# A transformer block on one core: a lead of 24 row-maxima tiles, filled in feed-forward turns 5 to 7, and the first sequence's projections a tile later

## The chip, the core and the metric

One core of one Trainium2 chip runs the whole program. Its engines are TensorE (PE in the profile, with its weight loads as PEld), VectorE (DVE), ScalarE (ACT), GpSimd (POOL) and the queue of SyncE (SP) that issues the DMAs. The metric is the device time of one execution, in microseconds; lower is better.

## What is computed

Eight sequences of 512 tokens and 256 channels pass through a feed-forward half step, an attention with 16 heads of 16 channels and an ALiBi bias, and the same feed-forward half step again:

```python
def _L0_ffn_ref(x, w_gate, w_up, w_down):
    gate = jnp.einsum('bsd,hd->bsh', x, wg)
    up = jnp.einsum('bsd,hd->bsh', x, wu)
    h = jax.nn.silu(gate) * up
    return jnp.einsum('bsh,dh->bsd', h, wd)
...
scores = jnp.einsum('bhld,bhsd->bhls', qh, kh) * inv_sqrt_d + bias[None]
attn = jax.nn.softmax(scores, axis=-1)
...
x = x + 0.5 * _L0_ffn_ref(_layernorm(x, axis=-1), L0_ffn_w_gate, L0_ffn_w_up, L0_ffn_w_down)
x = x + _L0_attn_ref(_layernorm(x, axis=-1), L0_attn_Wq, L0_attn_Wk, L0_attn_Wv, L0_attn_Wo, L0_attn_bo)
x = x + 0.5 * _L0_ffn_ref(_layernorm(x, axis=-1), L0_ffn_w_gate, L0_ffn_w_up, L0_ffn_w_down)
```

## The kernel before

The program has three stages, each of eight turns, one for each sequence `b`: the first feed-forward (`w` = 0), the attention, and the second feed-forward (`w` = 1). The order of the work is written out by hand for every engine, and semaphores join the engines.

**A feed-forward turn** (PE: `ffn_turn`, `gate_up`, `down`) has six tiles `f` of 128 hidden channels. For each, PE makes gate and up (eight products of 128x512), ACT applies Silu (`gated`, L560), DVE multiplies (`hid`, L759), and ACT and POOL split the result into a rounded and a rest part (L554, L459). Then come the down products, half of them, the eight transposes of the next turn's rows (`turn_x`, L967), and the other half. Those transposes go into PSUM banks 4 and 5 (`turn_at`). In between DVE does the next sequence's layernorm: `ln_gather` and `ln_links` (a chain of small Newton steps, L683 to L693), `ln_apply` (`xn`, L700) and `keep` (L707).

**An attention turn** has four quads `n` of four heads, and eight steps `s` in each. A step makes the scores of two heads against 128 keys (two products, from `q_aug` and `k_aug`), ACT's exponential (L647), POOL's multiplication with a table (L527), and in every second step the products with the values (`weigh_values`). Softmax needs the row maxima beforehand. They come from separate score tiles: `scores_for_max` makes a tile of 128 queries by 512 keys on PE, in turn in banks 4 and 5, and `row_maxima` reduces it on DVE (L824). A quad has 16 such tiles, a sequence 64. When a quad's sixteenth tile is reduced, DVE negates its 16 maxima in two small instructions (`negate`, L834 and L836). PE transposes them in the quad's `max` fill (L1011), ACT copies them to `max_row`, and two DMAs move them into `q_aug`, where the scores of that quad need them. A tile waits until DVE has reduced the tile two before it, which had the same bank.

**The lead.** The tiles run ahead of the scores: `MAX_LEAD` = 26 tiles ahead. The first 20 (`FIRST_MAX`) are made in the first feed-forward, in turns 6 and 7 (`FIRST_MAX_AT`, `FIRST_MAX_DOWN`), and sequence 0 makes three tiles a step until the lead is 26; from then on every step makes two.

```python
    ahead = MAX_LEAD + 2 * (step + 1)
    ahead = min(ahead, FIRST_MAX + 3 * (step + 1)) if b == 0 else ahead
```

**The fills** (`FILLS`, and `FIRST_AT` for sequence 0) are everything else of the attention on PE: transposes of the next rows (`xt`), projections (`qk`, `v`), transposes of heads and the output projection, at fixed steps; ACT drains each bank, and POOL or DVE splits it. Those of sequence 0 are done in turns 4 and 5 of the first feed-forward: its rows, kept in `heads` (L721), are transposed after a tile (`FIRST_TURN_AT`, L1079), ACT and DVE split them into `att_t` (L569, L776), and the first projections follow after later tiles.

Within attention step (n, s) DVE's order is: in quad 1, steps 2 to 5, one `xn` for a later sequence (`apply_kept`, L714), or for the last but one sequence the layernorm of sequence 0 (`first_rows`); then the maxima of the step, with a negation if a quad is complete; then `divide` (L888, L890) in step 4, or the split of `xt` (L880) in quad 0.

Of the kernel before, what the change touches and what calls it, by code (L numbers as in the profile page):

```python
# [82 lines left out]
def tables():  # L83
# [19 lines left out]
    for e in range(2):  # L103
# [25 lines left out]
FIRST_TURN_AT = (4, 0)  # L129
FIRST_AT = {(4, 3): "qk0_next", (4, 4): "qk1_next", (5, 0): "v0_next", (5, 1): "v1_next", (5, 2): "qk2_next", (5, 3): "qk3_next"}  # L130

FIRST_MAX_AT = {(B - 2, 0): range(0, 2), (B - 2, 2): range(2, 4), (B - 2, 4): range(4, 6),
                **{(B - 1, f): range(2 * f + 6, 2 * f + 8) for f in range(5)}}
FIRST_MAX_DOWN = {2: range(16, 18), 4: range(18, 20)}
FIRST_MAX = 20
# [17 lines left out]
MAX_LEAD = 26  # L153


def max_tiles_after(b, step):

    ahead = MAX_LEAD + 2 * (step + 1)
    ahead = min(ahead, FIRST_MAX + 3 * (step + 1)) if b == 0 else ahead
    return min(ahead, MAX_TILES) if b == B - 1 else ahead  # L160


def max_tiles_at(b, step):

    return range(max_tiles_after(b, step - 1), max_tiles_after(b, step))
# [30 lines left out]
def build_program(nc, d_x, d_wgu, d_wdn, d_watt, d_bo, d_qb, d_kb, d_diag, d_eye, d_scale, d_out):  # L196
    d_qrows = nc.dram_tensor("q_rows_scratch", (2, 2 * NSEG, NP, L), F32).ap()
    d_krows = nc.dram_tensor("k_rows_scratch", (ROWS - ROW_BIAS, L), F32).ap()
    with ExitStack() as ctx:
# [242 lines left out]
        def _(pool):  # L442
# [9 lines left out]
            def split_hidden(w, b):  # L452
# [10 lines left out]
                if w == 1 and first(b):  # L463
                    take(B, TAIL_AT[FT - 1])
                if w == 0 and first(b):
                    lay_ones()
# [79 lines left out]
        def _(act):  # L546
            def ffn_turn(w, b):
# [24 lines left out]
                hidden_hi(FT - 1)  # L572
                if w == 1 and first(b):
                    drain(B, TAIL_AT[FT - 1])
# [84 lines left out]
        def _(dve):  # L659
# [78 lines left out]
            def ffn_turn(w, b):  # L738
# [10 lines left out]
                for f in range(FT):  # L749
# [11 lines left out]

                    if f == 0 and w == 0 and not first(b):
                        ln_stats(1, b - 1, 2)
                        ln_stats(1, b - 1, 3)
# [8 lines left out]
                    if w == 0 and (b, f - 2) == FIRST_TURN_AT:  # L773
                        for k in range(KC):
                            dve.wait_ge(first_hi, k + 1)
                            nc.vector.tensor_tensor(att_t[:, 1, k, :], ps[:, turn_at + k, :], att_t[:, 0, k, :].bitcast(F32),  # L776
                                                    ALU.subtract).then_inc(first_split, 1)
# [175 lines left out]
        def _(pe):  # L953
# [25 lines left out]
            def fill(b, name, halves=(0, 1)):  # L979
# [27 lines left out]
                elif kind == "max":  # L1007
                    if halves[0] == 0:
                        pe.wait_ge(neg_ready, seq * NQ + part + 1)
                    if halves[0] == 0:  # L1010
# [22 lines left out]
            def scores_for_max(b, tiles):  # L1033

                for tile in tiles:
# [10 lines left out]
                    if seq == 0 and tile == 2 * STEPS:  # L1046
                        pe.wait_ge(drained, fill_no(-1, "max0_next") + 1)
# [163 lines left out]
```

## Time and profile before

| | |
|---|---|
| median of 3 runs | 893.54 us (890.49 to 893.92) |
| profiled execution | 892.85 us |
| its span | 891.1 us |
| mean granted clock | 0.97 |
| PE busy | 92% of the span |
| DVE busy | 73% |
| ACT, POOL busy | 58%, 48% |

The span goes from the first to the last instruction on the core. The granted clock is the share of TensorE's full clock of 2.4 GHz; 0.50 is the lower level of 1.2 GHz. A stretch from A to B is given in us from the start of the span: turn 4 goes from 104.86 to its down products at 125.40, quad 0 of sequence 0 from 197.43 to 223.32, quad 0 of sequence 3 from 406.13 and its quad 1 from 422.52 to 439.79, and quad 1 of sequence 4 from 488.30 to 506.77. PE 92% says that PE has something under way nearly always, not that it runs at its peak, and a share is a mean over three stages with different limits.

### The profile page before, as it was taken

What the parts mean: (1) busy time and instruction counts of PE and PEld (TensorE: products, weight loads), DVE (VectorE), ACT (ScalarE), POOL (GpSimd) and SP (SyncE); (2) the same over time, 40 slices, a digit from 0 to 9 for tenths busy, and PEclk for the clock granted to TensorE, in tenths of its full rate; (3) what the DMA queues carried; (4) which work ended last, traced back from release to release, by engine and by line L of the source; (5) the groups of instructions that cost most, each with busy time, mean ns of one, the idle gap of its engine ahead of it and who ended that gap; (6) DMA issues with size and microseconds to landing.
All of it is one profiled execution on the core that took longest, in us unless ns stands there. A gap on an engine that the chain in (4) does not pass through costs nothing.

```text
span 891.1 us, 13021 instructions
## 1 busy us (share of the span) xinstructions
PE 819.8 (92%) x4576; PEld 499.9 (56%) x4576; DVE 646.1 (73%) x1347; ACT 521.1 (58%) x745; POOL 425.6 (48%) x486
## 2 busy tenths in 40 slices
PE   2699989997899999999999999999899988999997
PEld 2578878763354453453444444444443436888886
DVE  5588877885787777777777777777878716777764
ACT  4343444334677777677777677677577773344443
POOL 0343345352544744744745645745554545344433
PEclk9799999996899999999999999999899999999999
DMA  9230015302532531531441541540522000010001
GB/s 362 103 40 3 2 29 78 41 11 31 72 50 26 72 54 21 72 54 20 72 60 15 73 60 15 72 66 12 69 43 31 2 3 1 32 44 26 26 25 50
DMA packets 21491, 43.18 MB, mean 48 GB/s; under 512 B 3848, under 2 KB 5912, under 8 KB 21208
## 3 DMA queue, kind: packets, MB, share of 16 engines
q1 hardware_dynamic: 21400, 41.92, 27.5%
q8 instruction: 63, 1.03, 0.5%
q14 instruction: 28, 0.23, 0.1%
HBM read 12.02 MB, written 4.62 MB: 19 GB/s over the span
## 4 chain that ended last, share of the span: by engine, by line
PE 65%; DVE 18%; DMA 4%; ACT 4%; issue 4%; POOL 2%; SPq 2%; DVEq 0%; ACTq 0%
PE ps L955 60%; DVE row_max L824 7%; DVE hid L759 3%; DMA q_aug<-max_row 2%; DMA q_scale<-q_scale 2%; PE ps L1016 2%; ACT stage L605 2%; PE ps L967 1%; DVE xnt L880 1%; ACT xnt L611 1%; DVE newton L691 1%; DVE xn L714 1%; DVE var L683 1%; PE ps L993 1%; POOL x_sb L510 1%
## 5 line engine op out<-in xcount | busy, mean ns | idle before, releaser
L824 DVE TENSOR_REDUCE row_max<-ps 128x1 f32<-128x512 f32 x512 | 329.3, 685 | 105.9 <-PE ps L955 104.5
L647 ACT ACTIVATE probs<-ps 128x1024 f32<-128x1024 f32 x256 | 259.9, 1026 | 48.9 <-PE ps L955 48.4
L527 POOL TENSOR_TENSOR probs<-probs,diag 128x256 f32<-128x256 f32 x256 | 186.5, 732 | 193.6 <-ACT probs L647 193.5
L459 POOL TENSOR_TENSOR hid_r<-hid,hid_r 128x512 fp32r<-128x512 f32 x96 | 124.8, 1301 | 196.1 <-ACT hid_r L554 195.2
L955 PE MATMUL ps<-xnt,wgu_r 128*128 128x512 f32 x768 | 195.8, 409 | 17.3 <-DVE hid L759 13.0
L955 PE MATMUL ps<-k_aug,q_aug 60*128 60x512 f32 x512 | 163.5, 448 | 19.6 <-DVE row_max L824 14.6
L955 PEld LDWEIGHTS ps<-xnt,wgu_r 128*128 128x128 f32 x768 | 145.9, 194 | 59.2 <-DVE hid L759 18.2
L955 PE MATMUL ps<-probs,v_aug 128*32 128x512 f32 x1024 | 141.9, 627 | 7.0 <-POOL probs L527 7.0
L560 ACT ACTIVATE gated<-ps 128x512 f32<-128x512 f32 x96 | 57.3, 598 | 141.4 <-PE ps L955 132.2
L955 PE MATMUL ps<-q_aug,k_aug 62*128 62x512 f32 x512 | 131.3, 505 | 3.8 <-DMA q_aug<-max_row 3.4
L955 PEld LDWEIGHTS ps<-k_aug,q_aug 60*128 60x128 f32 x512 | 81.0, 190 | 73.1 <-DVE row_max L824 66.5
L955 PEld LDWEIGHTS ps<-q_aug,k_aug 62*128 62x128 f32 x512 | 49.1, 187 | 116.1 <-issue 70.6
L759 DVE SCALAR_TENSOR_TENSOR hid<-ps,gated 128x512 f32<-128x512 f32 x96 | 65.9, 687 | 56.4 <-PE ps L955 28.7
L955 PE MATMUL ps<-wdn_r,hid_r 128*128 128x256 f32 x768 | 97.4, 282 | 0.9 <-ACT stage L605 0.9
L955 PEld LDWEIGHTS ps<-wdn_r,hid_r 128*128 128x128 f32 x768 | 93.8, 188 | 3.0 <-issue 1.6
L605 ACT COPY stage<-ps 128x512 f32<-128x512 f32 x96 | 56.3, 586 | 52.6 <-PE ps L955 28.9
L554 ACT CAST hid_r<-hid 128x512 fp32r<-128x512 f32 x96 | 59.1, 615 | 21.3 <-DVE hid L759 21.2
L483 POOL TENSOR_TENSOR parts<-stage,parts 128x512 fp32r<-128x512 f32 x32 | 41.2, 1286 | 35.7 <-ACT parts L611 35.7
L955 PEld LDWEIGHTS ps<-probs,v_aug 128*32 128x32 f32 x1024 | 20.4, 109 | 47.2 <-issue 24.7
L955 PE MATMUL ps<-xnt,wqkv 128*128 128x512 f32 x168 | 46.6, 413 | 0.0
L700 DVE TENSOR_SCALAR xn<-x_sb,mean_var,rstd 128x256 f32<-128x256 f32 x64 | 38.2, 622 | 0.5
L663 DVE BATCH_NORM_STATS2 stats<-x_sb 128x6 f32<-128x256 f32 x96 | 34.1, 410 | 5.4 <-DMA x_sb<-x_in 5.4
(72 smaller groups left out, 656.9 us busy)
## 6 DMA issues: line engine op xcount, KB each, us to landing
q_aug<-parts SPq DMA_DIRECT2D x96, 128.0 KB, 4.2
k_aug<-parts SPq DMA_DIRECT2D x96, 128.0 KB, 6.0
x_sb<-x_in SPq DMA_DIRECT2D x8, 512.0 KB, 12.7
x_out<-x_sb SPq DMA_DIRECT2D x8, 512.0 KB, 2.6
diag<-diag_table SPq DMA_DIRECT2D x1, 2048.0 KB, 18.8
wgu_i<-w_gate_up SPq DMA_DIRECT2D x2, 768.0 KB, 6.0
w_att<-w_att SPq DMA_DIRECT2D x1, 1024.0 KB, 11.2
q_aug<-max_row SPq DMA_DIRECT2D x64, 8.0 KB
```

What stands on the lines that cost most here:

```text
L459: nc.gpsimd.tensor_tensor(hid_r[:, 1, f, :], hid[:, f % 2, :], hid_r[:, 0, f, :].bitcast(F32), ALU.subtract).then_inc(s["hid_lo"], 1)
L483: nc.gpsimd.tensor_tensor(lo, stage[:, slot_of(b, name), :], hi.bitcast(F32), ALU.subtract).then_inc(done[SPLIT_POOL], 1)
L527: nc.gpsimd.tensor_tensor(tile, tile, diag[:, kt % 2, n * QH + 2 * pair:n * QH + 2 * pair + 2, :], ALU.mult).then_inc(fixed, 1)
L554: nc.scalar.copy(hid_r[:, 0, f, :], hid[:, f % 2, :]).then_inc(s["hid_hi"], 1)
L560: nc.scalar.activation(gated[:, f % 2, :], ps[:, gate_at + f % 2, :], ACT.Silu, scale=DEQ).then_inc(s["gated_ready"], 1)
L605: nc.scalar.copy(stage[:, slot_of(b, name), :], bank).then_inc(drained, 1)
L647: nc.scalar.activation(probs[:, kt % 2, 2 * pair:2 * pair + 2, :], ps[:, at:at + 2, :], ACT.Exp, scale=SLOPE_UNITS[pair]).then_inc(exp_don ...
L663: nc.vector.bn_stats(stats[:, slot, tile, :], x_of(b, tile)).then_inc(ln_step, 1)
L700: nc.vector.tensor_scalar(xn[:, tile, :], x_of(b, tile), mean_var[:, 0, tile, 0:1], rstd[:, 0, tile:tile + 1], ALU.subtract, ALU.mult).the ...
L759: nc.vector.scalar_tensor_tensor(hid[:, f % 2, :], ps[:, up_at + f % 2, :], DEQ, gated[:, f % 2, :], ALU.mult, ALU.mult).then_inc(s["hid_r ...
L824: nc.vector.reduce_max(row_max[:, quad % 2, u % 2, u // STEPS, (u % STEPS) // 2:(u % STEPS) // 2 + 1], max_bank(tile), mybir.AxisListType. ...
L955: return nc.tensor.matmul(out, lhs, rhs, start=start, stop=stop, **k)
```

## The change

Four things, on several engines:

1. `FIRST_TURN_AT` goes from (4, 0) to (4, 1), and the first two projections of sequence 0 from after tiles 3 and 4 to after tiles 4 and 5 of turn 4. POOL and ACT get a place for the drain of a fill after a turn's last tile.
2. DVE's half of that split comes straight after `hid` of tile 3, ahead of the layernorm's links; before, it came after `hid` of tile 2 and the links behind that.
3. `MAX_LEAD` is 24, and all of it is made in the first feed-forward: two tiles after the last tile of turn 5, six in turn 6, twelve after the six tiles of turn 7 and four among its down products. No step makes three tiles.
4. The first transpose of maxima waits until the tiles before the down products are reduced, since their bank is its own.

```diff
-FIRST_TURN_AT = (4, 0)
-FIRST_AT = {(4, 3): "qk0_next", (4, 4): "qk1_next", (5, 0): "v0_next", (5, 1): "v1_next", (5, 2): "qk2_next", (5, 3): "qk3_next"}
+FIRST_TURN_AT = (4, 1)
+FIRST_AT = {(4, 4): "qk0_next", (4, 5): "qk1_next", (5, 0): "v0_next", (5, 1): "v1_next", (5, 2): "qk2_next", (5, 3): "qk3_next"}
...
-FIRST_MAX_AT = {(B - 2, 0): range(0, 2), (B - 2, 2): range(2, 4), (B - 2, 4): range(4, 6),
-                **{(B - 1, f): range(2 * f + 6, 2 * f + 8) for f in range(5)}}
-FIRST_MAX_DOWN = {2: range(16, 18), 4: range(18, 20)}
-FIRST_MAX = 20
+FIRST_MAX_AT = {(B - 3, 5): range(0, 2), (B - 2, 0): range(2, 4), (B - 2, 2): range(4, 6), (B - 2, 4): range(6, 8),
+                **{(B - 1, f): range(2 * f + 8, 2 * f + 10) for f in range(FT)}}
+FIRST_MAX_DOWN = {2: range(20, 22), 4: range(22, 24)}
...
-MAX_LEAD = 26
...
+MAX_LEAD = 24
...
-    return range(max_tiles_after(b, step - 1), max_tiles_after(b, step))
+    made = MAX_LEAD + 2 * step
+    return range(made, min(made + 2, MAX_TILES) if b == B - 1 else made + 2)
...
                     nc.vector.scalar_tensor_tensor(hid[:, f % 2, :], ps[:, up_at + f % 2, :], DEQ, gated[:, f % 2, :],
                                                    ALU.mult, ALU.mult).then_inc(s["hid_ready"], 1)
 
+                    if w == 0 and (b, f - 2) == FIRST_TURN_AT:
+                        for k in range(KC):
+                            dve.wait_ge(first_hi, k + 1)
+                            nc.vector.tensor_tensor(att_t[:, 1, k, :], ps[:, turn_at + k, :], att_t[:, 0, k, :].bitcast(F32),
+                                                    ALU.subtract).then_inc(first_split, 1)
...
+                        if b < 0:
+                            pe.wait_ge(s1_used, FIRST_MAX_DOWN[2][0])
```

How the orders move. In turn 4, DVE, from `hid` of tile 2 on. Before:

```order
L759 SCALAR_TENSOR_TENSOR hid<-ps,gated 128x512
L691 TENSOR_TENSOR newton<-newton,var 128x8
L693 SCALAR_TENSOR_TENSOR rstd<-newton,rstd 128x8
L689 SCALAR_TENSOR_TENSOR newton<-rstd 128x8
L691 TENSOR_TENSOR newton<-newton,var 128x8
L693 SCALAR_TENSOR_TENSOR rstd<-newton,rstd 128x8
L776 TENSOR_TENSOR att_t<-ps,att_t 128x512 x2
L759 SCALAR_TENSOR_TENSOR hid<-ps,gated 128x512
```

And after the change, from the same `hid`, which is L756 there:

```order
L756 SCALAR_TENSOR_TENSOR hid<-ps,gated 128x512
L688 TENSOR_TENSOR newton<-newton,var 128x8
L690 SCALAR_TENSOR_TENSOR rstd<-newton,rstd 128x8
L686 SCALAR_TENSOR_TENSOR newton<-rstd 128x8
L688 TENSOR_TENSOR newton<-newton,var 128x8
L690 SCALAR_TENSOR_TENSOR rstd<-newton,rstd 128x8
L756 SCALAR_TENSOR_TENSOR hid<-ps,gated 128x512
L762 TENSOR_TENSOR att_t<-ps,att_t 128x512 x2
```

The two splits of `att_t` have moved behind the `hid` of tile 3.

At the end of turn 5, DVE, after the last `xn`. After the change:

```order
L697 TENSOR_SCALAR xn<-x_sb,mean_var,rstd 128x256
L704 TENSOR_SCALAR kept_mean<-mean_var 128x4
L704 TENSOR_SCALAR kept_rstd<-rstd 128x4
L821 TENSOR_REDUCE row_max<-ps 128x1 x2
L660 BN_STATS stats<-x_sb 128x6 x4
L726 TENSOR_TENSOR xnt<-ps,xnt 128x512 x2
```

The pair of reductions is new there; the rest is the order of before.

In every attention turn, DVE, in quad 1, from its `xn` of step 2 to its `xn` of step 5. Before:

```order
L714 TENSOR_SCALAR xn<-x_sb,kept_mean,kept_rstd 128x256
L824 TENSOR_REDUCE row_max<-ps 128x1 x2
L834 TENSOR_SCALAR max_in<-row_max 128x2x8
L836 SCALAR_TENSOR_TENSOR max_in<-row_max,max_in 128x2x8
L714 TENSOR_SCALAR xn<-x_sb,kept_mean,kept_rstd 128x256
L824 TENSOR_REDUCE row_max<-ps 128x1 x2
L714 TENSOR_SCALAR xn<-x_sb,kept_mean,kept_rstd 128x256
L824 TENSOR_REDUCE row_max<-ps 128x1 x2
L888 RECIPROCAL den<-stage 128x16
L890 TENSOR_TENSOR heads<-stage,den 128x4x64
```

After the change:

```order
L711 TENSOR_SCALAR xn<-x_sb,kept_mean,kept_rstd 128x256
L821 TENSOR_REDUCE row_max<-ps 128x1 x2
L711 TENSOR_SCALAR xn<-x_sb,kept_mean,kept_rstd 128x256
L821 TENSOR_REDUCE row_max<-ps 128x1 x2
L831 TENSOR_SCALAR max_in<-row_max 128x2x8
L833 SCALAR_TENSOR_TENSOR max_in<-row_max,max_in 128x2x8
L711 TENSOR_SCALAR xn<-x_sb,kept_mean,kept_rstd 128x256
L821 TENSOR_REDUCE row_max<-ps 128x1 x2
L885 RECIPROCAL den<-stage 128x16
L887 TENSOR_TENSOR heads<-stage,den 128x4x64
```

The negation (L834 and L836, now L831 and L833) stands behind the maxima of step 3 instead of those of step 2. It does so in all four quads.

## Rows read from the trace of the kernel before

**Rows 1.** The page, busy time, share of the span and instructions by engine.
```profile
PE 819.8 (92%) x4576; PEld 499.9 (56%) x4576; DVE 646.1 (73%) x1347; ACT 521.1 (58%) x745; POOL 425.6 (48%) x486
```
**Rows 2.** The page, the chain that ended last, shares by engine.
```profile
PE 65%; DVE 18%; DMA 4%; ACT 4%; issue 4%; POOL 2%; SPq 2%; DVEq 0%; ACTq 0%
```
**Rows 3.** Stretches: width; busy PE, PEld, DVE, ACT, POOL; PEclk, DMA share, GB/s.
```profile
104.86:125.40 20.54, 16.90 (x70) 13.08 (x69) 13.43 (x38) 7.85 (x15) 5.17 (x4) 0.92 0.01 2
197.43:223.32 25.89, 19.90 (x78) 8.12 (x77) 16.56 (x28) 11.09 (x15) 5.50 (x9) 0.74 0.28 34
406.13:422.52 16.39, 15.43 (x85) 6.74 (x85) 12.04 (x22) 11.94 (x17) 7.14 (x13) 1.00 0.00 1
422.52:439.79 17.27, 16.40 (x97) 7.71 (x93) 14.00 (x25) 12.54 (x17) 13.04 (x16) 1.00 0.62 93
488.30:506.77 18.47, 17.59 (x96) 7.78 (x93) 13.99 (x25) 12.55 (x17) 13.05 (x16) 0.91 0.63 87
```
**Rows 4.** Timeline of turn 4: start, duration, engine, work, idle time before and its releaser.
```profile
107.66 1.09 PE L1079 MATMUL ps<-eye,heads 128*128 128x128 f32 x8 [0.77 <-DVE heads L721]
115.87 1.28 DVE L776 TENSOR_TENSOR att_t<-ps,att_t 128x512 fp32r<-128x512 f32 x2
117.20 2.43 PE L955 MATMUL ps<-att_t,wqkv 128*128 128x512 f32 x6 [2.86 <-DVE att_t L776]
119.43 2.85 PE L955 MATMUL ps<-xnt,wgu_r 128*128 128x512 f32 x8
122.12 1.57 PE L955 MATMUL ps<-att_t,wqkv 128*128 128x512 f32 x6
123.53 2.03 PE L955 MATMUL ps<-xnt,wgu_r 128*128 128x512 f32 x8
```
**Rows 5.** Timeline, end of turn 5, and a pair of reductions in turn 6.
```profile
151.59 1.04 PE L967 MATMUL ps<-eye,xn 128*128 128x128 f32 x8
152.47 0.16 DVE L707 TENSOR_SCALAR kept_rstd<-rstd 128x4 f32<-128x4 f32 x1
168.71 1.27 DVE L824 TENSOR_REDUCE row_max<-ps 128x1 f32<-128x512 f32 x2
```
**Rows 6.** Timeline, turn 7, from tile 5 to the down products.
```profile
190.33 0.27 PE L1011 MATMUL ps<-eye,max_in 128*32 128x128 f32 x1
190.37 0.69 DVE L759 SCALAR_TENSOR_TENSOR hid<-ps,gated 128x512 f32<-128x512 f32 x1 [0.19 <-PE ps L955]
```
**Rows 7.** Timeline, PE, steps 0 and 1 of sequence 0.
```profile
199.45 0.49 PE L955 MATMUL ps<-k_aug,q_aug 60*128 60x512 f32 x1 [1.28 <-DVE row_max L824]
203.18 0.79 PE L955 MATMUL ps<-k_aug,q_aug 60*128 60x512 f32 x1 [1.96 <-DVE row_max L824]
```
**Rows 8.** Timeline, sequence 3, quad 0, steps 2 to 4.
```profile
412.06 0.17 DVE L834 TENSOR_SCALAR max_in<-row_max 128x16 fp32r<-128x16 f32 x1
412.27 0.17 DVE L836 SCALAR_TENSOR_TENSOR max_in<-row_max,max_in 128x16 f32<-128x16 f32 x1
413.80 2.56 DVE L824 TENSOR_REDUCE row_max<-ps 128x1 f32<-128x512 f32 x4
415.25 0.73 POOL L527 TENSOR_TENSOR probs<-probs,diag 128x256 f32<-128x256 f32 x1
```
**Rows 9.** Timeline, sequence 3, quad 1, steps 2 to 5.
```profile
429.25 0.65 DVE L836 SCALAR_TENSOR_TENSOR max_in<-row_max,max_in 128x16 f32<-128x16 f32 x1
430.52 1.33 POOL L483 TENSOR_TENSOR att_t<-stage,att_t 128x512 fp32r<-128x512 f32 x1
432.61 1.27 DVE L824 TENSOR_REDUCE row_max<-ps 128x1 f32<-128x512 f32 x2
433.34 1.09 PE L955 MATMUL ps<-k_aug,q_aug 60*128 60x512 f32 x2
```
**Rows 10.** Timeline, sequence 3, quad 2, the reductions of steps 3 and 4.
```profile
447.20 1.29 DVE L824 TENSOR_REDUCE row_max<-ps 128x1 f32<-128x512 f32 x2 [0.56 <-PE ps L955]
448.85 1.29 DVE L824 TENSOR_REDUCE row_max<-ps 128x1 f32<-128x512 f32 x2 [0.37 <-PE ps L955]
```

More of the change, by code:

```diff
@@ L152 @@
 MAX_TILES = 2 * NQ * STEPS
-MAX_LEAD = 26
[L156 to L160, printed above, removed]
+MAX_LEAD = 24
 def max_tiles_at(b, step):
-    return range(max_tiles_after(b, step - 1), max_tiles_after(b, step))
+    made = MAX_LEAD + 2 * step
+    return range(made, min(made + 2, MAX_TILES) if b == B - 1 else made + 2)
 SPLIT_POOL, SPLIT_DVE, HEADS, OUT = ("qk", "turn"), ("xt",), ("heads",), ("out",)
@@ L464, in split_hidden @@
                     take(B, TAIL_AT[FT - 1])
+                if w == 0 and (b, FT - 1) in FIRST_AT:
+                    take(-1, FIRST_AT[b, FT - 1])
                 if w == 0 and first(b):
@@ L572, in ffn_turn @@
                 hidden_hi(FT - 1)
+                if w == 0 and (b, FT - 1) in FIRST_AT:
+                    drain(-1, FIRST_AT[b, FT - 1])
                 if w == 1 and first(b):
@@ L772, in ffn_turn @@
                         keep(at, b - 1, 1)
[L773 to L777, printed above, removed]
                     if w == 0 and (b, f) in FIRST_MAX_AT:
@@ L1045, in scores_for_max @@
                         pe.wait_ge(drained, fill_no(-1, "qk3_next") + 1)
-                    if seq == 0 and tile == 2 * STEPS:
+                    if seq == 0 and tile == FIRST_MAX_DOWN[2][0]:
                         pe.wait_ge(drained, fill_no(-1, "max0_next") + 1)
```

## The prediction

> **What bounds the kernel now.** I read first the page's busy shares: PE has 92% of the span and DVE 73% [rows 1], so time is won or lost where PE stands still or is slowed, and DVE matters where PE waits for it. The chain that ended last says the same, 65% PE and 18% DVE [rows 2]. Busy time by stretches comes next [rows 3]. Quad 0 of sequence 0, the first stretch of the attention, takes 25.89 us at a granted clock of 0.74. The same quad of sequence 3 takes 16.39 us at 1.00, with more fills in it. Feed-forward turn 4, as far as its down products, takes 20.54 us at 0.92, while DVE is busy for 13.43. These are the places that the change aims at. Everything else that it moves is in the negations, so last I followed DVE in the timeline round three of them.
>
> The sum is made against the profiled execution: span 891.1, time 892.85. The median of the runs shown is 893.54, 0.69 more, and I add that at the end. About 0.5% (4.5 us) is what a measurement of this kernel can tell from no change.
>
> **Turn 4: transposes after f=1, first projection after f=4, the split ahead of the Newton links.** Now PE waits 0.77 for the rows of sequence 0, then 2.86 for the split `att_t`, and after that wait it runs at the lower level (1.2 GHz of 2.4): six products take 2.43 and eight 2.85, against 1.57 and 2.03 for the same work at the higher one [rows 4]. Together 0.77 + 2.86 + 0.86 + 0.82 = 5.3. After the change the rows have been ready for a turn's tile, and the split follows `hid` of f=3 directly. PE has the eight products of f=4 in between, 2.03 long as those at 123.53; DVE needs 1.28 for the two splits behind `hid`, and may start late by the links of f=2. I leave a wait of 0.5: **-4.8** (ends -3.5, were the links as late as now, and -5.3).
>
> **Turn 5: two tiles after f=5.** The transposes of turn 6 go into the same PSUM banks, so they now wait until DVE has reduced both tiles. Those two reductions stand behind `kept_mean` and `kept_rstd`, the last of which starts at 152.47 and takes 0.16; with 1.27 for a pair of reductions they end at about 153.9. The transposes start at 151.59 now [rows 5]. The two score products, ahead of the down products, are inside that wait. **+2.4** (ends 0.5, the products alone, and 3.0). Behind the transposes wait ACT's and DVE's halves of `xnt` and then gate and up of turn 6; those have the second half of the down products as cover, and would add the time of a reduction pair if it were too short.
>
> **Turn 7: two tiles after f=5, and the first transpose of the maxima behind them.** That transpose (L1011) writes the bank of those tiles and newly waits for 20 reductions. DVE's `hid` of f=5 starts at 190.37 and takes 0.69 [rows 6], a pair of reductions 1.27 more, so PE is let go at about 192.4 instead of 190.33. With rounding and semaphores **+2.2** (ends 0.5 and 2.6). Behind it on PE are all down products of the turn. SP's move of the maxima shifts with it and still lands before the attention starts.
>
> **Quad 0 of sequence 0: two tiles a step instead of three.** PE waits for the third tile's bank, 1.28 in step 0 and 1.96 in step 1, and behind the second wait a product takes 0.79 against 0.49 before: the lower level of the clock [rows 7]. Six such tiles leave the quad, each a product on PE and a reduction on DVE. I followed the steps with durations of the rows: DVE stays the one that is waited for in steps 1 to 5 (two splits of `xnt` wait for ACT), and the quad comes out at 16.9 us with the clock up. It isn't likely to stay up: steps 0 to 2 still hold no value products, and PE stands still for about 1.3 us for tiles 28 and 29. I add 2.5 for slow stretches and take 19.4, so **-6.5**. Ends: -9.0 with the clock up, -2.9 if it behaves as now.
>
> **Every quad: the negation goes from step 2 to step 3.** A lead of 24 makes the sixteenth tile of a quad in step 3. The first instruction of a negation takes 0.17 when POOL is idle, and so does the second; reductions, which read PSUM, keep 0.64 under POOL's operations too [rows 8]. But where POOL is under way the second takes 0.65, and it ends as POOL's operation ends [rows 9]. `xn` (L714) waits in the same way. So a negation costs what is left of POOL's operation.
> - Quad 0: in step 2 it sits in a gap in which DVE waits for ACT's half of `xt1`; it costs nothing there. In step 3 it falls between four reductions that follow one another, under POOL's operations, the last of them until 415.98 [rows 8]. The reductions of step 4 start 0.9 later; PE, which needs them in step 5, catches up a part at step 6, where it waited for DVE before. +0.4, seven times: 2.8.
> - Quad 1: DVE loses the negation ahead of step 3's reductions, which PE does not need so early (its value products wait for POOL there), and gets it ahead of step 4's. Those start at 432.61 now, and PE issues step 5's first tile at 433.34 right behind the first of them [rows 9]. If the first half just misses the start of POOL's 1.33 us operation at 430.52, they start 0.8 later; if it catches it, not at all. By my times it misses by 0.05. +0.6 for each of sequences 0 to 5: 3.6.
> - Quads 2 and 3: DVE is idle for 0.56 between step 2's negation and step 3's reductions, and for 0.37 ahead of step 4's [rows 10]. The negation now has to go into those 0.37, and needs 0.34 alone and more under POOL. +0.2, fourteen times: 2.8.
> - Sequence 6, quad 1, where the negation is ahead of a long chain: -0.3. Sequence 7, quad 1: +0.2. Two more tiles in step 19 of the last sequence, otherwise bound by ACT: +0.3.
>
> Together **+9.4**. Ends: 1.5, if DVE's slack covers nearly all, and 15. What holds DVE off in these rows is POOL's operation, to its end. The Trainium skill, GPSIMD Engine Reference, "1. Specifications", says only that GpSimd's SBUF interfaces are shared with those VectorE instructions that have two SBUF inputs or run in a two-port mode, and names no turn-taking. Priced by that sentence without the rows, a moved negation would be its own 0.34, largely inside the gaps, and the sum of this part 3 instead of 9.4. The trace agrees with the page on which instructions suffer and goes beyond it on how long.
>
> **Sum.** -4.8 + 2.4 + 2.2 - 6.5 + 9.4 = +2.7; 892.85 + 2.7 = 895.6, and with the 0.69 of the median **896.3**.
>
> **The rivals.**
> - *Faster: DVE's slack covers the negations.* Quad 1's negation catches the boundary, the other quads absorb theirs, and sequence 0 starts with the clock up. For it: PE's waits for reductions are short in most steps, and 0.05 us decide in quad 1. Against: the gap of 0.37 in quad 2 is shorter than the negation with its wait. -4.8 + 2.4 + 2.2 - 9.0 + 1.5 = -7.7: 885.8.
> - *Slower: quad 1 loses the clock.* With step 5's tiles held by the negation, PE has a second weak stretch right behind the one at POOL's wait in step 3. Quad 1 of sequence 4 shows what follows: 18.47 us at 0.91 against 17.27 at 1.00 in sequence 3 [rows 3], 1.2 us. It decides once quad 1's wait before step 5 grows by about 0.8. Three more sequences so, and the quad late every time (2.5 more): +2.7 + 3.6 + 2.5 = +8.8: 902.3.
> - *The start doesn't come free.* Quad 0 of sequence 0 keeps its slow stretches, since DVE's wait for ACT's halves of `xnt` stays: -2.9 instead of -6.5, so +6.3: 899.8. The wait for three tiles was then not what set those steps.
>
> **How the numbers follow.** Forecast 0.38, the faster rival 0.28, quad 1's clock 0.22, the start 0.12. The forecast lies within 0.5%; the two rivals above it are slower by more. So faster 0.28, same 0.38, slower 0.34. The likeliest case's own range is 889 to 898.5; the range over all goes to a little beyond both outer rivals, 885 to 904. The clock falls in other places too (sequences 2, 4 and 6 now), and these may come or go by 3 us with no cause in the change; it is inside the range.
>
> **What would show it.** Turn 4 to its down products near 15.7 us. A PE wait of some 2 us before turn 6's transposes, and one of 1.6 before the first L1011 (L1010 there). Quad 0 of sequence 0 between 17 and 20 us. Quad 0 of sequences 1 to 6 at 16.8 instead of 16.39, quad 1 at 17.3 to 18.2, quads 2 and 3 up by 0.2; negation instructions of 0.4 to 1.3 us in step 3. If the steady quads are unchanged to 0.1, the forecast is wrong by the whole of its largest term and the kernel is faster. If quad 0 of sequence 0 is over 23 us, the extra tile wasn't what slowed it.

## The result and the profile after

| | time, us | clock of the runs |
|---|---|---|
| before, 4 runs beside it | 892.01 (889.68 to 893.92) | |
| after, 4 runs | 901.7 (898.82 to 907.14) | 0.967, 0.967, 0.958, 0.961 |
| after, the profiled execution | 898.82, span 896.9 | 0.967 |

The ratio is 1.0121, with a 95% interval of 1.0076 to 1.0167: the change makes the kernel slower. Ten more runs, made later and told below (e11), gave 897.38 us and 1.0053 (1.0029 to 1.0078). So the forecast of 896.3 lies 5.4 us under the first measurement and 1.1 under the second, and both lie in the range of 885 to 904; only the second lies in the likeliest case's own range, 889 to 898.5. As a difference from the kernel before the forecast does less well: +2.8 was forecast, and +9.7 and +5.2 were measured.

The page of the profile after, busy time by engine and the chain that ended last, against [rows 1, 2]:

```profile
PE 823.9 (92%) x4576; PEld 500.8 (56%) x4576; DVE 645.0 (72%) x1347; ACT 519.7 (58%) x745; POOL 426.5 (48%) x486
PE 61%; DVE 25%; DMA 4%; issue 4%; ACT 3%; SPq 2%; POOL 1%; DVEq 0%; ACTq 0%
```

All counts of instructions are the same, and DVE works no longer. Yet the chain goes through DVE for 25% of the span instead of 18%: work has moved to where it is waited for.

The stretches of the profile after, with the columns of [rows 3] (width; busy PE, PEld, DVE, ACT, POOL; granted clock, DMA share, GB/s). In order: turn 4; turn 7 before and after the first transpose of the maxima; quad 0 of sequence 0; quads 0 and 1 of sequence 1, then of sequence 3:

```profile
104.92:120.69 15.77, 15.13 (x71) 12.01 (x70) 14.05 (x40) 8.00 (x15) 6.14 (x5) 1.00 0.01 2
186.00:189.60 3.60, 1.91 (x10) 1.12 (x9) 2.62 (x5) 1.72 (x3) 2.40 (x3) 1.00 0.02 5
189.60:193.00 3.40, 3.40 (x19) 3.17 (x17) 0.00 (x0) 1.54 (x2) 3.19 (x5) 0.50 0.02 5
197.95:216.23 18.28, 15.66 (x72) 6.53 (x72) 12.72 (x22) 10.88 (x15) 5.54 (x9) 0.81 0.40 48
264.91:281.66 16.75, 15.65 (x88) 6.66 (x85) 12.45 (x22) 12.04 (x18) 7.71 (x14) 1.00 0.01 2
281.66:299.44 17.78, 16.02 (x97) 7.53 (x93) 14.52 (x25) 12.45 (x17) 13.20 (x16) 1.00 0.69 89
400.16:418.34 18.18, 17.16 (x85) 6.83 (x85) 12.38 (x22) 11.95 (x17) 7.20 (x14) 0.91 0.01 2
418.34:436.11 17.77, 16.02 (x97) 7.52 (x93) 14.50 (x25) 12.45 (x17) 13.17 (x16) 1.00 0.67 90
```

Turn 4 has lost 4.77 us and has its full clock. Quad 0 of sequence 0 has lost 7.61, though its clock is still 0.81. Against that, a steady quad 0 takes 16.75 in sequence 1 at full clock and 18.18 in sequence 3, where the clock is 0.91 (before: 16.39 at 1.00). All of sequences 2 to 6 look like sequence 3: 18.16 to 18.21. Quad 1 takes 17.78 in place of 17.27 and keeps its clock in sequences 1 to 5 (in sequence 6, where it had lost it before, it takes 22.96 at 0.78 against 22.35 at 0.85). And turn 7, which had no such stretch before, has 3.4 us at the lower level.

**Where the 5.8 us of span went**, by the starts of the sequences (the first exponential of each) in the two profiled executions:

| part | before | after | difference | predicted |
|---|---|---|---|---|
| up to sequence 0 | 197.4 | 197.9 | +0.5 | -0.2 |
| sequence 0 | 75.8 | 67.0 | -8.8 | about -5.5 |
| sequences 1 to 6 | 402.4 | 412.9 | +10.5 | about +7.5 |
| sequence 7 | 50.2 | 52.7 | +2.5 | about +0.9 |
| after it | 165.3 | 166.4 | +1.1 | 0 |

What sequences 1 to 7 lose is more than what the freed start had saved. Of the other three executions after, one was as long as this one, and two were longer, at lower clocks (0.958 and 0.961).

**The steps in the trace.** The timeline of the profile after (start, duration, engine, work, idle time before and its releaser), turns 4, 5 and 7:

```profile
114.59 1.28 DVE L762 TENSOR_TENSOR att_t<-ps,att_t 128x512 fp32r<-128x512 f32 x2
115.93 1.66 PE L952 MATMUL ps<-att_t,wqkv 128*128 128x512 f32 x6 [0.64 <-DVE att_t L762]
...
146.59 1.25 DVE L704 TENSOR_SCALAR kept_mean<-mean_var 128x4 f32<-128x4 f32 x1
147.75 0.16 DVE L704 TENSOR_SCALAR kept_rstd<-rstd 128x4 f32<-128x4 f32 x1
147.82 1.27 DVE L821 TENSOR_REDUCE row_max<-ps 128x1 f32<-128x512 f32 x2
149.20 1.06 PE L964 MATMUL ps<-eye,xn 128*128 128x128 f32 x8 [1.54 <-issue]
...
187.95 1.28 DVE L821 TENSOR_REDUCE row_max<-ps 128x1 f32<-128x512 f32 x2
189.38 0.27 PE L1010 MATMUL ps<-eye,max_in 128*32 128x128 f32 x1 [1.70 <-DVE row_max L821]
189.40 3.61 PE L952 MATMUL ps<-wdn_r,hid_r 128*128 128x256 f32 x16
```

The split in turn 4 now costs PE 0.64 instead of 2.86 [rows 4]. In turn 5 PE stands still for 1.54 us until the pair of reductions is through, and that pair stands behind a copy of four numbers a row that took 1.25 us. In turn 7 PE waits 1.70 us. The sixteen down products behind it took 3.61, at the lower level.

The same view, DVE, POOL and PE in steps 3 to 5 of sequence 3, quad 0 and then quad 1, against [rows 8, 9]:

```profile
409.13 0.20 DVE L831 TENSOR_SCALAR max_in<-row_max 128x16 fp32r<-128x16 f32 x1
409.27 0.73 POOL L522 TENSOR_TENSOR probs<-probs,diag 128x256 f32<-128x256 f32 x1
409.37 0.66 DVE L833 SCALAR_TENSOR_TENSOR max_in<-row_max,max_in 128x16 f32<-128x16 f32 x1
409.96 1.27 DVE L821 TENSOR_REDUCE row_max<-ps 128x1 f32<-128x512 f32 x2
...
426.38 1.32 DVE L831 TENSOR_SCALAR max_in<-row_max 128x16 fp32r<-128x16 f32 x1
426.38 1.28 POOL L478 TENSOR_TENSOR att_t<-stage,att_t 128x512 fp32r<-128x512 f32 x1
427.73 0.65 DVE L833 SCALAR_TENSOR_TENSOR max_in<-row_max,max_in 128x16 f32<-128x16 f32 x1
428.63 1.28 DVE L821 TENSOR_REDUCE row_max<-ps 128x1 f32<-128x512 f32 x2
429.36 1.10 PE L952 MATMUL ps<-k_aug,q_aug 60*128 60x512 f32 x2 [0.84 <-DVE row_max L821]
```

In quad 0 the second negation instruction runs from 409.37 to 410.03 and ends with POOL's operation, at 410.00. In quad 1 the first starts together with POOL's 1.28 us operation and takes 1.32: it just missed the boundary, as the prediction had it. The reductions of step 4 start at 428.63, and PE waits 0.84 for them.

What this does to PE is seen best in a quad 0 at full clock. PE, from step 4's transposes on, in sequence 3 before and in sequence 1 after:

```profile
416.14 0.50 PE L955 MATMUL ps<-q_aug,k_aug 62*128 62x512 f32 x2
416.48 0.42 PE L955 MATMUL ps<-k_aug,q_aug 60*128 60x512 f32 x2
416.83 1.07 PE L955 MATMUL ps<-probs,v_aug 128*32 128x512 f32 x8
418.04 0.50 PE L955 MATMUL ps<-q_aug,k_aug 62*128 62x512 f32 x2
```

```profile
275.00 0.50 PE L952 MATMUL ps<-q_aug,k_aug 62*128 62x512 f32 x2
275.51 1.09 PE L952 MATMUL ps<-k_aug,q_aug 60*128 60x512 f32 x2
276.53 1.07 PE L952 MATMUL ps<-probs,v_aug 128*32 128x512 f32 x8
277.74 0.50 PE L952 MATMUL ps<-q_aug,k_aug 62*128 62x512 f32 x2
```

The value products start 1.53 us after step 5's scores instead of 0.69, because the two maxima tiles ahead of them (`k_aug`) are issued as reductions free their banks. Step 5 takes 2.74 instead of 1.90; step 6 gives back 0.55.

What PE did ahead of a fall is seen in the stretch from step 4's scores to step 5's value products: in sequence 3 after, where the clock fell at 411.5, inside step 5; in sequence 1 after, where it did not; and in sequence 3 before (columns as above):

```profile
407.53:411.88 4.35, 3.57 (x16) 1.51 (x12) 4.25 (x10) 3.08 (x4) 1.77 (x4) 0.95 0.00 0
272.36:276.53 4.17, 3.39 (x16) 1.52 (x12) 4.07 (x9) 2.99 (x4) 1.76 (x3) 1.00 0.01 2
413.50:416.83 3.33, 2.69 (x16) 1.42 (x12) 2.85 (x5) 2.15 (x4) 1.75 (x3) 1.00 0.00 0
```

The same twelve products (the count of PE takes in four that are just ending) take 0.84 us longer in sequence 1 than before (4.17 against 3.33), with no value products among them. Sequence 1 has this thin stretch and keeps its clock, so the stretch by itself doesn't decide whether the clock falls.

### The profile page after: what moved, and what is told of

Same layout as the page of the kernel before. It is cut to its first block, busy times and chain, and to the rows that moved or that the text cites. A ratio compares the mean times of both kernels' runs of the same rounds, so it can differ in the third digit from the quotient of the medians.

```text
span 896.9 us, 13022 instructions
## 1 busy us (share of the span) xinstructions
PE 823.9 (92%) x4576; PEld 500.8 (56%) x4576; DVE 645.0 (72%) x1347; ACT 519.7 (58%) x745; POOL 426.5 (48%) x486
## 3 DMA queue, kind: packets, MB, share of 16 engines
q1 hardware_dynamic: 21400, 41.92, 27.3%
## 4 chain that ended last, share of the span: by engine, by line
PE 61%; DVE 25%; DMA 4%; issue 4%; ACT 3%; SPq 2%; POOL 1%; DVEq 0%; ACTq 0%
PE ps L952 57%; DVE row_max L821 12%; DVE hid L756 3%; DMA q_aug<-max_row 2%; DMA q_scale<-q_scale 2%; DVE max_in L831 2%; PE ps L964 1%; ACT stage L602 1%; DVE max_in L833 1%; DVE xnt L877 1%; ACT xnt L608 1%; DVE newton L688 1%; DVE xn L711 1%; PE ps L1010 1%; PE ps L990 1%
## 5 line engine op out<-in xcount | busy, mean ns | idle before, releaser
L952 PEld LDWEIGHTS ps<-k_aug,q_aug 60*128 60x128 f32 x512 | 78.4, 191 | 75.4 <-DVE row_max L821 62.9
L756 DVE SCALAR_TENSOR_TENSOR hid<-ps,gated 128x512 f32<-128x512 f32 x96 | 65.8, 687 | 51.4 <-PE ps L952 31.7
L660 DVE BATCH_NORM_STATS2 stats<-x_sb 128x6 f32<-128x256 f32 x96 | 34.1, 409 | 5.5 <-DMA x_sb<-x_in 5.5
```

Of the source, the lines that this page charges most:

```text
L660: nc.vector.bn_stats(stats[:, slot, tile, :], x_of(b, tile)).then_inc(ln_step, 1)
L756: nc.vector.scalar_tensor_tensor(hid[:, f % 2, :], ps[:, up_at + f % 2, :], DEQ, gated[:, f % 2, :], ALU.mult, ALU.mult).then_inc(s["hid_r ...
L952: return nc.tensor.matmul(out, lhs, rhs, start=start, stop=stop, **k)
```

## The experiments

Eleven kernels and the change once more, all with 6 to 12 runs each. Nearly every one was slower or faster partly by its clock, so I use one measure beside the ratio. Every run has a span and a mean granted clock; **slow time** is what it spent at the lower level, 2 x span x (1 - clock). Over the 74 runs of the kernel before that stood beside the experiments, a microsecond of slow time goes with 0.32 us of span; within the runs of all kernels together with 0.34. Span less a third of the slow time, the **rest**, then varies by only 0.4 to 1.3 us (standard deviation) within a kernel. The third is fitted to these runs and no law; the clock is given to 0.001, which is 1.8 us of slow time. A fall in a steady quad 0 costs more than a third, 1.5 us for 3.4 (18.18 against 16.68), so the rest of a kernel with many such falls still holds some clock.

| kernel | runs | ratio | mean span | slow time | rest |
|---|---|---|---|---|---|
| before | 74 | 1 | 890.4 | 50.5 | 873.6 |
| after, first measurement | 4 | 1.0121 | 900.4 | 66.2 | 878.4 |
| after, again (e11) | 10 | 1.0053 | 896.0 | 54.5 | 877.8 |
| turn 4 alone (e1) | 12 | 0.9947 | 886.0 | 48.4 | 869.9 |
| negation late, lead 26 (e2) | 6 | 1.0137 | 901.8 | 66.2 | 879.8 |
| late in quad 0 alone (e9) | 6 | 1.0116 | 900.9 | 67.3 | 878.5 |
| late in quad 1 alone (e10) | 12 | 1.0024 | 893.1 | 53.0 | 875.5 |
| change with lead 26 (e3) | 6 | 0.9904 | 882.3 | 34.1 | 870.9 |
| e3 with both waits cut (e8) | 6 | 0.9903 | 881.5 | 35.3 | 869.7 |
| change, negation in step 4 (e4) | 12 | 0.9969 | 887.3 | 37.4 | 874.9 |
| change without turn 5's pair (e5) | 7 | 1.0066 | 895.8 | 54.0 | 877.8 |
| change, pair ahead (e6) | 12 | 1.0040 | 894.0 | 52.5 | 876.5 |
| change, transpose later (e7) | 12 | 1.0012 | 892.1 | 48.5 | 876.0 |
| change, e6 and e7 together (e12) | 12 | 1.0021 | 892.4 | 49.1 | 876.1 |

### The change taken apart

**e1: only turn 4's part, on the kernel before.** The six lines of `FIRST_TURN_AT`, `FIRST_AT` and the split and drain that belong to them; 20 tiles and lead 26 stay.

> The kernel before with the change's turn 4 alone (transposes after f=1, the split behind hid of f=3, the first projections after f=4 and f=5). Main theory: turn 4 to its down products goes from 20.5 us to 15.7, as in the changed kernel, nothing else moves, so about 887.2 us against 892.0, ratio 0.995, with 1 us either way by where the clock falls. Rival (turn 4's gain is lost to what follows it): the attention starts as late as before and the ratio is 1.00.

888.08 us, ratio 0.9947 (0.9928 to 0.9966). The attention starts at 192.8 instead of 197.4. Quad 0 of sequence 0 is no shorter, 27.3. The part is worth what was predicted (-4.8; measured -4.5 on the median), and all of it reaches the end.

**e2: only the negation a step later, on the kernel before.** Lead 26 stays, so nothing but the place of two small DVE instructions changes:

```diff
-                        row_maxima(b, max_tiles_at(b, n * STEPS + s))
+                        row_maxima(b, max_tiles_at(b, n * STEPS + s), False)
+                        if s == 3 and not (last(b) and n == NQ - 1):
+                            negate(b * NQ + n + 1, (n + 1) % 2)
```

> The kernel before, lead 26, with one thing altered: each negation of the attention stands behind the maxima of step 3 instead of step 2, where the tile is complete. Main theory (the place of the negation on DVE is what costs, not the lead): quad 0 of sequences 1 to 6 goes from 16.4 to 16.75 us at full clock and to 18.2 where the clock falls, quad 1 from 17.3 to 17.8, together 7 to 12 us, 899 to 904 us, ratio 1.008 to 1.014. Rival (the shorter lead costs, since tiles and negation come later against the scores that need them, or the waits put into turns 5 and 7): the steady quads stay at 16.4 and 17.3 and the ratio is within 1.002.

903.43 us, ratio 1.0137 (1.0094 to 1.0181): 10.9 us for moving two instructions of 0.17 us per quad. At full clock quad 0 takes 16.7 and quad 1 17.8, as in the change, and quads 2 and 3 are unchanged at 16.1. The rest is up 6.2 us. The other part is clock: 15.7 us more of slow time. Its profiled execution, the fastest of the six, shows only one fall in a quad 0 (sequence 2, 19.7 us), so where the others lost their clock is not seen here; e9 shows it better.

**e3: the change, but with lead 26.** The first 24 tiles as in the change, then three tiles in steps 0 and 1 of sequence 0, so that a quad's sixteenth tile stays in step 2 and the negation with it:

```diff
-MAX_LEAD = 24
+MAX_LEAD = 26
+FIRST_MAX = 24
...
+    ahead = MAX_LEAD + 2 * (step + 1)
+    ahead = min(ahead, FIRST_MAX + 3 * (step + 1)) if b == 0 else ahead
```

> The changed kernel with its first 24 tiles and turn 4 kept, but lead 26: steps 0 and 1 of sequence 0 make three tiles, all later ones two, so that every negation is back behind step 2. Main theory: steady quads as before (16.4, 17.3, falls of the clock as before), the first feed-forward as in the changed kernel (attention starts near 198), quad 0 of sequence 0 near 19.5 us against 25.9: 892.0 + 0.5 - 6.4 = 886, ratio 0.993. Rival (the negations are innocent; three tiles a step or the turns' waits cost): quad 0 of sequence 0 back over 23 us and 890 or more, or steady quads still at 18.2.

884.26 us, ratio 0.9904 (0.9875 to 0.9933), the best of the study together with e8. Its stretches (quad 0 of sequence 0; quads 0 and 1 of sequence 3):

```profile
198.25:218.06 19.81, 15.79 (x76) 6.86 (x75) 13.99 (x24) 11.00 (x15) 5.54 (x9) 0.83 0.36 45
398.32:414.71 16.39, 15.43 (x83) 6.73 (x84) 12.04 (x22) 11.92 (x17) 7.08 (x13) 1.00 0.01 2
414.71:431.96 17.25, 16.39 (x95) 7.70 (x91) 13.98 (x25) 12.57 (x17) 13.04 (x16) 1.00 0.69 93
```

The steady quads are those of before [rows 3], and the long quad 0 of the start is gone: 19.8 instead of 25.9, with the three-tile steps still in it. So it was four more steps of three tiles that made it long, and the change's lead of 24 isn't needed for the gain. Against e1 the slow time is 14 us less and the rest 1 us more. Put together, e3 and e2 give 0.9904 x 1.0137 = 1.004 for the whole change (an estimate, which leaves out the tail's +1.4 us and the two three-tile steps that e3 still has): the second measurement of the change has that in its interval, the first doesn't.

**e4: the change, negation behind step 4's maxima.** The diff of e2 on the changed kernel, with `s == 4`.

> The changed kernel, lead 24, with each negation of the attention behind the maxima of step 4, ahead of divide, still ahead of the fill in step 5 that needs it. Main theory: in quad 0 DVE waits for ACT at that place anyway, so quad 0 is back at 16.4 us without a fall of the clock; quad 1 is freed ahead of step 4's maxima and pays ahead of step 5's instead, 17.3 to 17.7; together 8 us less than the changed kernel, about 892 to 894, ratio 1.000 to 1.003. Rival (the lead is what costs): quad 0 stays at 16.75 to 18.2 and the time near 901.

889.68 us, ratio 0.9969 (0.9950 to 0.9989), faster than expected. In sequence 3 quad 0 is back at 16.4 and quad 1 at 17.4; quad 2 takes 16.5 in place of 16.15. So step 3 is the bad place, and a lead of 24 doesn't need it. It isn't free, though: quad 2 of sequence 7 still takes 13.43 instead of 12.06, by the two more tiles that a shorter lead leaves for the end, and e4 stays 5.4 us over e3.

### Which quad

**e9 and e10: the negation late in one quad only, on the kernel before.** In e9 the test of e2 reads `n == 0`, in e10 `n == 1`, and the other quads negate in step 2.

> The kernel before (lead 26), with the two negation instructions moved behind step 3's maxima in quad 0 alone; in quads 1 to 3 they stay in step 2. Theory (the 0.3 us that quad 0 loses in steps 5 and 6, on top of the kernel's other waits, is what lets the clock fall there): quad 0 takes 16.7 at full clock and up to 19.6 with a fall, quad 1 stays at 17.3, and at least half of the slowdown of the full move (1.0137) is seen, ratio 1.006 to 1.010. Rival (quad 1's loss of 0.5 us under GpSimd's long operation carries it): ratio under 1.003.

> The kernel before (lead 26), with the two negation instructions moved behind step 3's maxima in quad 1 alone. Theory: quad 1 takes 17.8 (from 17.3), that is 7 x 0.5 = 3.5 us or 0.4%, and no more, as the falls of the clock belong to quad 0: ratio 1.003 to 1.005. Rival (quad 1 loses the clock by itself, the slower rival of the prediction): ratio 1.008 or above, with falls in quad 1's steps 5 and 6 in most sequences.

e9: 902.75 us, 1.0116 (1.0084 to 1.0149). e10: 894.74 us, 1.0024 (1.0005 to 1.0043). Stretches of e9 (quad 0 of sequences 1 and 2, quad 1 of sequence 2) and of e10 (quads 0 and 1 of sequence 1, then of sequence 2):

```profile
275.11:291.94 16.83, 15.69 (x88) 6.65 (x84) 12.56 (x22) 12.11 (x18) 7.77 (x14) 1.00 0.01 2
341.30:359.45 18.15, 17.15 (x84) 6.84 (x84) 12.41 (x22) 11.66 (x16) 7.25 (x13) 0.91 0.01 2
359.45:376.95 17.50, 16.46 (x95) 7.73 (x92) 14.26 (x25) 12.83 (x18) 13.10 (x16) 1.00 0.71 92
```

```profile
272.97:289.51 16.54, 15.44 (x88) 6.73 (x85) 12.19 (x22) 12.10 (x18) 7.80 (x14) 1.00 0.01 2
289.51:308.03 18.52, 17.05 (x97) 7.56 (x93) 14.55 (x25) 12.45 (x17) 13.06 (x16) 0.91 0.66 86
340.23:356.62 16.39, 15.44 (x83) 6.73 (x83) 12.03 (x22) 11.65 (x16) 7.21 (x13) 1.00 0.01 3
356.62:374.67 18.05, 16.33 (x95) 7.58 (x91) 14.84 (x25) 12.74 (x18) 13.10 (x16) 1.00 0.69 89
```

Quad 0 decides. With only 0.3 us lost there at full clock (0.85 in sequence 7) it brings 16.8 us of slow time more and nearly the whole slowdown of e2; in its profile quad 0 took 18.2 in sequences 2, 3, 5 and 6, at 0.91 in each. That is more than my theory gave it (1.006 to 1.010). Its rest is up by 4.9 where those losses at full clock make 2.7, since these falls cost more than a third. Quad 1, which loses 0.5 us at full clock, brings 2.5 us of slow time; the clock fell in it in sequences 1 and 5 (18.5 and 18.5), and in sequences 2 and 4 of the kernel before (18.2 and 18.5). So quad 1 is not where the slowdown comes from, as the slower rival had it. What quad 1 does when quad 0 is late as well, as in the change, these two don't show.

### The waits in the feed-forward

**e5: the change without turn 5's pair**, with 22 tiles in the feed-forward turns and three tiles in steps 0 and 1 of sequence 0.

> The changed kernel without the pair of maxima tiles in turn 5 (22 tiles in the feed-forward turns, three tiles instead of two in steps 0 and 1 of sequence 0, lead still 24). My theory of turn 5 (the pair and the wait of the next turn's transposes cost about +2.2 there): attention starts at about 195.8 us instead of 197.95, and quad 0 of sequence 0 takes 18.9 instead of 18.3, so the ratio to the kernel before is about 0.2% under the change's 1.0121, near 1.010. Rival (the wait in turn 5 hides in turn 6 or 7): the start stays at 197.9 and the ratio is 1.012 or above. Both: the clock still falls once in quad 0 of nearly every later sequence, since the negation is where the change puts it.

897.05 us, 1.0066 (1.0035 to 1.0098). The attention starts at 194.2, earlier than my 195.8 (no fall in turn 7 here), and quad 0 of sequence 0 takes 19.6, for my 18.9. In its profile the clock fell in quad 0 of sequences 2, 4, 5 and 7, not of nearly all. The rest equals that of the change: what turn 5 saves, the three-tile steps cost.

**e6: the pair's reductions ahead of the two copies.**

```diff
-                    if 1 in slots and f == 5:
-                        keep(at, b - 1, 1)
                     if w == 0 and (b, f) in FIRST_MAX_AT:
                         row_maxima(0, FIRST_MAX_AT[b, f])
+                    if 1 in slots and f == 5:
+                        keep(at, b - 1, 1)
```

> The changed kernel with the turn-5 pair's row maxima put ahead of the two copies of kept mean and reciprocal on VectorE (0.6 to 1.3 us of queue). Theory (the maxima wait behind the copies, and TensorE waits for the maxima): the idle stretch ahead of turn 5's transposes goes from 1.54 us to about 0.2, attention starts at about 196.6, and the whole is 1.3 us shorter than the change. Rival (another wait, such as the drain of v0_next or GpSimd's port, takes the place): the idle stretch is 1 us or more still.

Timeline of e6, turn 5:

```profile
146.45 1.28 DVE L821 TENSOR_REDUCE row_max<-ps 128x1 f32<-128x512 f32 x2
147.65 0.16 DVE L704 TENSOR_SCALAR kept_mean<-mean_var 128x4 f32<-128x4 f32 x1
147.72 1.25 DVE L704 TENSOR_SCALAR kept_rstd<-rstd 128x4 f32<-128x4 f32 x1
147.83 1.07 PE L964 MATMUL ps<-eye,xn 128*128 128x128 f32 x8 [0.32 <-issue]
```

The idle time falls from 1.54 to 0.32, as expected, though the attention starts at 197.1 for my 196.6 (the clock fell in turn 7); the copies still take 1.25 between them, now with nobody waiting. 895.80 us, 1.0040 (1.0016 to 1.0064); the rest is 1.3 us under e11's.

**e7: the first transpose of the maxima one tile later** (`f == 1` instead of `f == 0` in `down`).

> The changed kernel with the transpose of sequence 0's first maxima one f-tile later in turn 7's down products (f = 1 instead of f = 0). Theory (that transpose waits 1.7 us for the last row maxima, and the idle stretch with the products around it brings the clock to 0.5 for 3.4 us): the wait is under 0.8 us, the stretch at 189.6 to 193.0 is at full clock, and attention starts 1.5 to 2.5 us sooner (about 195.9). Rival A (the clock falls for another reason, such as the small products of turn 7): the wait shrinks and the fall stays, attention starts about 1 us sooner. Rival B (moving rows is late then): quad 0 of sequence 0 takes over 18.5 us.

Timeline of e7, turn 7:

```profile
188.04 1.20 PE L952 MATMUL ps<-wdn_r,hid_r 128*128 128x256 f32 x8
189.81 0.27 PE L1010 MATMUL ps<-eye,max_in 128*32 128x128 f32 x1 [0.56 <-DVE row_max L821]
```

The wait is 0.56 instead of 1.70 and no fall follows; the attention starts at 195.98. 894.26 us, 1.0012 (0.9988 to 1.0036), the rest 1.8 us under e11's. But the absence of the fall doesn't show that the wait caused it: e11, with the wait as it was, has none in turn 7 either, and e6 has one.

**e8 and e12: both edits together**, on e3 and on the change.

> The version with lead 26, 24 tiles made in the feed-forward turns and the later turn 4 (measured 0.9904 of the kernel before), with the turn-5 maxima ahead of the copies and the transpose of the first maxima one f-tile later. If both waits are what they seem, another 1.3 and 1.5 to 2.5 us go: about 881 us, ratio 0.987. If the start of the attention part only waits for something else then (rows that move, first maxima), the ratio stays at 0.990. The steady quads stay at 16.4 and 17.3, with no fall of the clock in quad 0.

> The changed kernel (lead 24) with both edits on waits: turn 5's row maxima ahead of the two copies, and the transpose of the first maxima one f-tile later in turn 7. If the gains add, attention starts 3 to 3.5 us sooner than in the change (about 194.7) and the ratio is 1.004 or less below that of the change measured beside it by at least 0.35%. If the time in the later part goes by where the falls of the clock land, the ratio can be anywhere from 0.998 to 1.007 whatever the start gained.

e8: 883.22 us, 0.9903 (0.9868 to 0.9937), 1.0 us under e3 and no difference that these runs can tell; the expected 881 wasn't reached. e12: 894.73 us, 1.0021 (0.9999 to 1.0044); its attention starts at 194.5, 3.5 us before that of the change's first profile and 1.5 before that of e11 (196.0), its rest is 1.7 us under e11's, and it is no better than e7 alone. The gains of the two don't add up in the time, and I didn't find out why.

**e11: the change again.**

> The changed kernel as it is, again, beside the others on the same chip. Its ratio was 1.0121 from four runs with 1.0 to 1.3% spread, while the three variants of it that shorten the wait in turn 5 or 7 by 1 to 4 us gave 1.0012 to 1.0066. If the variants gained by more than their own waits (fewer falls of the clock later on), this run gives 1.009 or above; if the first measurement lay high, 1.006 to 1.009.

897.38 us (894.36 to 903.55), 1.0053 (1.0029 to 1.0078): below both ranges that I had set. The rest is the same as in the first measurement to 0.6 us, the slow time 12 us less. Its profiled execution shows the falls otherwise placed. Stretches, quad 0 of sequences 2 and 3, quads 0 and 1 of sequence 4:

```profile
327.70:347.23 19.53, 18.61 (x83) 7.71 (x83) 12.38 (x22) 11.66 (x16) 7.43 (x13) 0.83 0.01 2
397.57:414.25 16.68, 15.62 (x83) 6.65 (x83) 12.38 (x22) 11.92 (x17) 7.21 (x14) 1.00 0.01 2
464.21:483.75 19.54, 18.59 (x83) 7.71 (x83) 12.37 (x22) 11.93 (x17) 7.35 (x14) 0.83 0.00 1
483.75:503.97 20.22, 18.56 (x95) 8.73 (x91) 14.50 (x25) 12.45 (x17) 13.24 (x16) 0.83 0.57 80
```

Here the clock falls for twice as long in quad 0, 6.8 us, and only in sequences 2, 4 and 5 (and for 3.4 in 7). And it falls in quad 1: for 6.8 us in sequences 4 and 5, where quad 1 takes 20.2, and for 17.1 in sequence 6, where it takes 24.9 against 22.35 before. The profiles of e5, e6 and e7, which have late negations in every quad too, also show falls in quad 1, in two to four of sequences 1 to 5; in e7 quad 1 of sequence 1 takes 20.5 right behind a quad 0 at full clock (16.8). So the slower rival's falls in quad 1 do come in the change, though not in every execution, and though e10 gives quad 1 by itself only 0.24%. No run has quads 0 and 1 late and the others not, so what the two do together isn't taken apart. The change has a cost at full clock and one that differs from execution to execution.

## Why the prediction was right and wrong

By its own steps, for the profiled executions:

- **Turn 4, -4.8: right.** 15.77 us to the down products for a forecast of 15.7; the wait for the split 0.64 for 0.5; e1 carries it to the end of the program.
- **Turn 5, +2.4: right in mechanism, a little high.** From the start of the down products to that of the transposes it is 4.63 us, against 2.84 before: +1.8, and 0.43 for the two score products, together +2.2. The term's copy of `kept_mean` stands where it was put, and e6, which moves it away, wins 1.3 in the rest.
- **Turn 7, +2.2: the wait was right, the clock was missed.** PE's wait of 1.70 was forecast as 1.6. Behind it sixteen down products took 3.61 us in place of the 2.15 that they take at full clock: another 1.45, which no term had. In e11 it didn't come.
- **Quad 0 of sequence 0, -6.5: right, and 1.1 too small**: 18.28 us for 19.4; 17.2 in e11, and 18.2 in e7.
- **The negation step, +9.4: the sum came out near, 11.8, and its make-up didn't.** (11.8 is +13.0 in sequences 1 to 7, less 1.2 in quads 1 to 3 of sequence 0.) At full clock the pieces add up to about 7 only (2.6 in quad 0, 2.9 in quad 1, 1.4 in the tail); that falls of the clock made up for what the term had too much is luck. *Quad 0* was given +0.4. At full clock it is +0.23 in sequence 1 (16.75 for 16.52), +0.29 in sequence 3 of e11 (16.68 for 16.39) and +0.86 in the last sequence, so the price of the wait holds. But in five sequences of the profile the clock fell in it, for 1.5 us more each (18.18 less 16.68), and e9 shows that this quad by itself makes the kernel 1.2% slower. *Quad 1*, +0.6, measured +0.5, by the mechanism named, to the boundary missed. *Quads 2 and 3*, +0.2 each, were unchanged to 0.1: steps 5 of quad 2 take 2.44 for 2.28, and step 6 gives the 0.16 back. The gap of 0.37 was shorter than the negation, and yet nobody waited long enough for it to count; 2.8 us of the term did not exist. *The tail*, +0.3, measured +1.4: quad 2 of sequence 7 takes 13.42 for 12.06, and step 19 itself, with two more tiles, 2.96 for 1.61. I had taken ACT for its bound.

So the step that failed, within a range that held, is one sentence long: that quad 0 costs what its late reductions cost. I had looked for a loss of the clock in quad 1, since quad 1 is where the kernel before shows one, and took quad 0's unbroken 1.00 [rows 3] as safety. In its step 5 PE issues the two maxima tiles as their banks come free, and the late reductions stretch just that place. That this is why the clock falls there is argued from the timeline; shown is only that it does. In sequences 1 to 7, the eight profiles with the late negation in quad 0 have one to five falls in a quad 0, the five with it in step 2 (before, e1, e3, e8, e10) have none, and e4's has one. The slower rival came near the first measurement with its 902.3, but by way of quad 1: e10 gives that quad 0.24%, and in the first profile of the change it lost its clock only in sequence 6, though in e11's in three sequences.

In microseconds of the table above: the change adds 4.4 us of rest (mean of its 14 runs, 878.0 against 873.6), for a forecast of +2.7, and slow time of 4 us in the second and 15.7 us in the first measurement, worth 1.3 and 5.2. The split is by the fitted third, so some clock is in the first part too. That part is nearly what a prediction from rows can hold. The second needed a wider right side of the likeliest case: I had allowed 3 us for falls that come and go, and they came with 5. That the full range held both measurements is owed to the rivals' prices, not to the forecast's mechanism.

Priced only by what the Trainium skill states in GPSIMD Engine Reference, "1. Specifications", that VectorE and GpSimd share SBUF interfaces, the term was 3 in the prediction's estimate, less than the 7 or so that it cost at full clock. The trace after bears out what the rows had added: a 128x16 instruction with SBUF operands alone (L831) took 1.32 us beside a POOL operation of 1.28, and a pair of reductions from PSUM 1.27 to 1.28 throughout.

## What to carry to other kernels

Before a small instruction is moved in a queue, ask what reads stand behind it and who waits for those, and price it by what is left of the other engine's operation, not by its own length. Then look at how the waiting engine's clock stands in that very place: a wait of 0.8 us, given back to 0.3 a step later, went with 1.2% here (e9), as it recurred in every sequence, and the clock fell there in four of the six from 1 to 6. And when a change is made of parts, run each part and the whole without it: here the better kernel was the change with one constant put back (0.9904).

## What the runs showed of the hardware that was not expected

- **The clock's falls can fall into step with the program.** In the profile of the change, quad 0's falls begin at 343.2, 411.5, 479.7, 548.0 and 616.2, 68.2 to 68.3 us apart, and the sequences between take 68.0 to 68.5. e12 has its own at 339.0, 407.3, 475.6, 543.8 and 612.1. In e11, with the same program as the first, they are twice as long and skip sequences. That the program's own period keeps the falls in place is my reading of these times; no run tests it.
- **The same program was 0.7% apart from one measurement to another**: 1.0121 and 1.0053. The kernel before gave 892.0 to 892.6 in the four that stood beside them. A span less a third of its slow time agreed between the two to 0.6 us.
- **A lost clock cost less than half of its time.** A fall of 3.4 us added 1.5 us to quad 0, and over 74 runs of the kernel before the span rose by 0.32 us per microsecond at the lower level. That part of the time at the lower level is waiting anyway would explain it; it isn't shown.
